# Second attention of a conv-attention network: scores computed a second time with keys on the partitions, exponentials summed in pairs

## The chip, the cores and the metric

The kernel runs as one program on one core of a Trainium2 chip. The metric is the time of one execution on the device in microseconds (us), as the median of several runs. PE is TensorE (matrix products), PEld its loading of weights, DVE is VectorE, ACT ScalarE, POOL GpSimd, and SP the engine that issues most transfers (its queue is SPq).

## What is computed

The input is x (2 images, 256 channels, 32x32 pixels, fp32). A first block (deformable attention and an MLP) gives a new x. The second block is plain multi-head attention over the 1024 pixels of an image, 8 heads of width 32, and it is the one that the change touches:

```python
def _L1_conv_ref(x, W_qkv, b_qkv, W_out, b_out):
    xf = jnp.transpose(x.reshape(B, C, N), (0, 2, 1))
    qkv = xf @ W_qkv + b_qkv
    qkv = qkv.reshape(B, N, N_HEADS, 3 * D_K)
    q, k, v = jnp.split(qkv, 3, axis=-1)
    attn = jnp.einsum('bihd,bjhd->bijh', q, k) * SCALE
    attn = jax.nn.softmax(attn, axis=2)
    res = jnp.einsum('bijh,bjhd->bihd', attn, v)
    res = res.reshape(B, N, N_HEADS * D_K)
    res = res @ W_out + b_out
    res = res + xf
```

Two images of eight heads give 16 heads (G), and the 1024 queries of a head are cut into 8 tiles of 128 rows (NK). One such tile of one head is a *unit*, so there are 128 units.

## The kernel before

Each engine has its own instruction list, written out by hand; semaphores order them across engines. An engine executes its list strictly in order, so what stands behind a waiting instruction waits too.

The second block runs in these steps. **Values:** PE makes V (L1026, 16 pieces) and DVE adds the bias and saves it (L741). **Projections:** PE makes Q and K in 8 pieces (L1038); ACT and DVE split each into two fp32r parts, high and low (L531, L767), and SP sends the parts to DRAM (`send_parts`, L299). Meanwhile DVE splits V into three 16-bit parts. **Head loads:** `load_head` (L303, L304) brings a head's parts back, stacked on the partitions in four groups of 32 rows (`Q_STACK`, `K_STACK`), so that one 128-row product sums high and low parts; eight transfers a head, into two buffers in turn.

**Units:** a loop of 8 rounds with 16 units each (PE: L1078). For a unit, PE computes the scores of 128 queries against 1024 keys into two PSUM banks (`scores`, L1047), DVE finds each row's negated maximum (`maxes`, L773), ACT takes the exponential with that maximum as its bias (`exps`, L535). The probabilities have queries on the partitions, and the product with V needs keys there, so PE transposes them (`turn`, L1055, eight 128x128 pieces). ACT and DVE copy them out of PSUM as two fp16 parts (L540, L543, L776, L779) and POOL makes one half of the low part (L390). PE multiplies both parts with V's three (`weigh`, L1063, 16 products); a column of ones beside V gives the sum. DVE inverts it (L786), ACT scales (L550), and POOL adds the three parts (L395, L397). The scores run three units ahead of the product with V.

**End:** PE transposes the results back to channels on the partitions (L1102), multiplies with W_out (L1113), DVE adds the residual (L814), SP stores.

## Time and profile before

| | |
|---|---|
| median of 3 runs | 1402.4 us (1402.36 to 1404.89) |
| the profiled execution | 1401.21 us |
| its span, first to last instruction | 1399.0 us |
| mean granted TensorE clock | 0.974 of full |
| busy: PE / PEld / DVE / ACT / POOL | 93% / 44% / 66% / 69% / 54% |

The span is what the trace shows, and the time of the same execution lies 2.2 us above it. Busy shares are averages over stages with different limits. A time of the trace is counted from the span's start. In rows of instructions, x8 is a merged group of 8, and a row's "idle before" names what ended the idle time. A product of two fp32 operands appears as two MATMUL records (L1038: 32 products in the code, x64 in the trace); a product of fp32r operands (L1047) or a transpose is one.

### The profile page before, as it was taken

How to read it: one execution, taken by the hardware profiler on the slowest of the kernel's cores; microseconds unless marked ns; L12 is line 12 of the kernel's file. 1: busy time of each engine (PE TensorE's matmuls, PEld its weight loads, DVE VectorE, ACT ScalarE, POOL GpSimd, SP SyncE). 2: the span in 40 equal slices, each digit the busy share in tenths (PEclk: the TensorE clock that was granted, in tenths of full speed). 3: DMA queues.
4: the chain of work that ended last, by engine and by line, in shares of the span. 5: the costliest groups of instructions: out<-in, count | busy, mean ns of one | idle time of the engine just before them, and what ended most of it. 6: DMA issues, size and time to landing. Idle time of an engine off the chain costs nothing.

```text
span 1399.0 us, 29958 instructions
## 1 busy us (share of the span) xinstructions
PE 1302.2 (93%) x11666; PEld 616.0 (44%) x11666; DVE 921.5 (66%) x1270; ACT 967.6 (69%) x1263; POOL 748.9 (54%) x681
## 2 busy tenths in 40 slices
PE   3169999999999999999999998799997999999998
PEld 2132222222222222222222226444454888888885
DVE  6876666666666666666666657410037999999995
ACT  3377777777777777777777773332204999999994
POOL 4166666666666666666666652200000767777772
PEclk9579999999999999999999999999999999999999
DMA  2141110111011101110111000000007222212211
GB/s 69 54 134 31 31 32 2 31 31 32 2 31 32 29 4 32 31 26 7 31 32 23 9 1 1 1 0 0 0 29 272 62 60 60 54 45 52 60 30 60
DMA packets 19922, 53.27 MB, mean 38 GB/s; under 512 B 4642, under 2 KB 7330, under 8 KB 19668
## 3 DMA queue, kind: packets, MB, share of 16 engines
q1 hardware_dynamic: 19824, 51.92, 14.1%
q8 instruction: 70, 1.15, 0.4%
q14 instruction: 24, 0.20, 0.0%
q10 hardware_dynamic: 4, 0.01, 0.0%
HBM read 40.95 MB, written 10.95 MB: 37 GB/s over the span
## 4 chain that ended last, share of the span: by engine, by line
PE 80%; DVE 11%; issue 3%; ACT 2%; POOL 2%; DMA 1%; SPq 1%; DVEq 0%; ACTq 0%; POOLq 0%
PE ps L898 31%; PE ps L907 17%; PE ps L889 5%; DVE aneg L773 5%; PE ps L1055 4%; PE ps L1063 4%; PE ps L1004 4%; PE ps L1014 4%; PE ps L1047 3%; DVE conv L620 2%; PE ps L1038 1%; DVE big L776 1%; POOL big L355 1%; PE ps L1026 1%; PE ps L991 1%
## 5 line engine op out<-in xcount | busy, mean ns | idle before, releaser
L898 PE MATMUL ps<-big,w 64*64 64x512 f32 x4096 | 483.5, 589 | 0.0
L479 ACT ACTIVATE big<-ps 128x1024 f32<-128x1024 f32 x256 | 262.0, 1023 | 179.0 <-PE ps L898 179.0
L674 DVE TENSOR_SCALAR big<-big 128x1024 f32<-128x1024 f32 x256 | 177.8, 694 | 263.8 <-POOL big L370 263.8
L668 DVE TENSOR_TENSOR big<-qpad,ps 128x1024 f32<-128x1024 f32 x256 | 311.0, 1215 | 7.8 <-ACT ps L458 5.4
L370 POOL TENSOR_TENSOR big<-qpad 128x1024 f32<-128x1024 f32 x128 | 244.5, 1910 | 133.2 <-PE ps L898 68.6
L370 POOL TENSOR_TENSOR big<-qpad,V 128x1024 f32<-128x1024 f32 x128 | 244.5, 1910 | 129.7 <-PE ps L898 73.5
L479 ACT ACTIVATE big<-ps,vec 128x1024 f32<-128x1024 f32 x256 | 284.0, 1109 | 0.0
L390 POOL TENSOR_TENSOR big<-BT,big 128x512 f16<-128x512 f32 x129 | 150.4, 1166 | 248.0 <-DVE big L776 248.0
L907 PE MATMUL ps<-big,w3s 128*32 128x512 f32 x2048 | 246.2, 598 | 1.3 <-ACT big L479 1.3
L898 PEld LDWEIGHTS ps<-big,w 64*64 64x64 f32 x4096 | 146.6, 133 | 205.9 <-issue 112.6
L773 DVE TENSOR_REDUCE aneg<-ps 128x1 f32<-128x1024 f32 x131 | 158.3, 1209 | 6.0 <-PE ps L1047 5.7
L535 ACT ACTIVATE big<-ps,aneg 128x1024 f32<-128x1024 f32 x130 | 148.5, 1142 | 6.0 <-DVE aneg L773 5.3
L1055 PE MATMUL ps<-ident,big 128*128 128x128 f32 x1032 | 136.3, 274 | 3.8 <-DVE big L779 3.8
L907 PEld LDWEIGHTS ps<-big,w3s 128*32 128x32 f32 x2048 | 53.5, 109 | 181.7 <-ACT big L479 92.2
L1055 PEld LDWEIGHTS ps<-ident,big 128*128 128x128 f32 x1032 | 121.1, 141 | 23.2 <-DVE big L779 5.7
L1063 PE MATMUL ps<-BT,big 128*128 x2048 | 115.6, 208 | 1.1
L1063 PEld LDWEIGHTS ps<-BT,big 128*128 128x128 f16 x2048 | 99.0, 97 | 21.3 <-issue 10.3
L889 PE MATMUL ps<-S,wl 57*64 57x512 bf16 x1024 | 102.3, 389 | 1.5 <-ACT vs L474 1.5
L1047 PE MATMUL ps<-h1l,h1h 128*128 128x512 f32 x262 | 94.5, 443 | 6.8 <-DMA h1l<-k_d 5.2
L889 PEld LDWEIGHTS ps<-S,wl 57*64 57x64 bf16 x1024 | 29.5, 105 | 144.7 <-ACT big L479 80.7
L779 DVE SCALAR_TENSOR_TENSOR big<-ps,big 128x512 f16<-128x512 f32 x129 | 89.1, 691 | 0.8 <-ACT big L543 0.4
L540 ACT ACTIVATE BT<-ps 128x512 f32<-128x512 f32 x129 | 79.1, 613 | 4.0 <-PE ps L1055 4.0
(140 smaller groups left out, 1116.5 us busy)
## 6 DMA issues: line engine op xcount, KB each, us to landing
raw<-s_f SPq DMA_DIRECT2D x32, 512.0 KB, 6.1
h1h<-q_d SPq DMA_DIRECT2D x64, 128.0 KB, 3.0
h1l<-k_d SPq DMA_DIRECT2D x64, 128.0 KB, 3.1
q_d<-XN SPq DMA_DIRECT2D x8, 512.0 KB, 2.6
k_d<-XN SPq DMA_DIRECT2D x8, 512.0 KB, 2.6
X<-in_x SPq DMA_DIRECT2D x2, 1024.0 KB, 6.3
out<-X SPq DMA_DIRECT2D x8, 256.0 KB, 2.0
m<-grid_d SPq DMA_DIRECT2D x1, 1024.0 KB, 4.6
```

Source lines behind the costliest of these rows:

```text
L370: pool.tensor_tensor(h1[m % HRING].rearrange("p (y a b) -> p y a b", y=2, b=W), u.unsqueeze(2).to_broadcast(shape), a[:, :, HALF // W * hf ...
L390: pool.tensor_tensor(PTL[u % 2][:, 0:HALF], PF[u % 2], PTH[u % 2][:, 0:HALF], ALU.subtract).then_inc(pFl_ready, 1)
L479: act.activation(h2[m % H2RING], z2[m % ZRING], ACT.Relu, bias=v("cb2") if m % 2 else 0.0).then_inc(h2_ready, 1)
L535: act.activation(PR[u % 2], bank(2 * (u % 2), 2), ACT.Exp, bias=aneg[u % 2][:, :]).then_inc(pr_ready, 1)
L668: dve.tensor_tensor(h1[m % HRING].rearrange("p (y a b) -> p y a b", y=2, b=W), u.unsqueeze(2).to_broadcast(shape), b[:, :, HALF // W * hf: ...
L674: dve.tensor_scalar(h1[m % HRING], h1[m % HRING], 0.0, None, ALU.max).then_inc(h1_ready, 1)
L773: dve.tensor_reduce(aneg[u % 2][:, :], bank(2 * (u % 2), 2), AX.X, ALU.max, negate=True).then_inc(mx_ready, 1)
L889: pe.matmul(z2[m % ZRING][CH * y:CH * (y + 1), HALF * x:HALF * (x + 1)], wl1[CH * x:CH * x + KROWS, 2 * w + y, :], S[CH * x:CH * x + KROWS ...
L898: last = pe.matmul(z2[m % ZRING][CH * y:CH * (y + 1), HALF * x:HALF * (x + 1)], w2[CH * x:CH * (x + 1), :], h1[m % HRING][CH * x:CH * (x + ...
L907: last = pe.matmul(zb[32 * k:32 * (k + 1), :], w3s[:, a:a + 32], h2[(m + k // 2) % H2RING][:, HALF * (k % 2):HALF * (k % 2 + 1)], start=(m ...
L1055: last = pe.transpose(bank(4 + hf)[:, P * i:P * (i + 1)], PR[u % 2][:, P * jt:P * (jt + 1)], ident[:, :])
L1063: last = pe.matmul(bank(6 + u % 2)[:, 0:VW], pT[u % 2][:, P * jt:P * (jt + 1)], V3[:, 2 * k + u // NK, jt, :], start=(jt == order[0] and p ...
```

## The change

The scores of a unit are now computed twice. `along(x)` computes them as before, queries on the partitions, only for the row maxima; its 128 queries are no longer consecutive but every eighth (`it:...:NK`), so that the maxima of a head lie in order in DRAM. POOL splits a head's maxima into two parts (`max_parts`), and SP moves them through DRAM into two more rows beneath the head's Q (`move_max`: a transfer out, a wait for it, a transfer in). K has ones in these two rows. `across(s)` then computes the scores with keys on the partitions, 128 keys against 1024 queries, and the two rows subtract each query's maximum within the product. ACT takes the exponential, which needs no transpose. PE multiplies V, as 32 columns, with it, in four products side by side, one for each quarter of the queries (`weigh`). POOL adds the exponentials of two units (`added`), and PE multiplies the sum with ones, again in four (`sums`). DVE divides once a head (`divide`), and SP puts the result in place (`place_head`, four transfers). All is fp32 there, without 16-bit parts.

The stack of a head's parts has three groups instead of four (the product of the two low parts is left out), so `load_head` issues six transfers. Q and K have three buffers (`HEADS3`) instead of two. `along` runs 13 units ahead (`AHEAD_MAX`) of `across` and has one pair of PSUM banks (0 and 1); `across` alternates between two pairs. The values are made between the first eight `along` and no longer before the projections. V's parts, the transposes, and the copies out of PSUM are gone. The loops are written out.

```diff
+        QS = [h1h[:, 2 * i:2 * i + 2, :].rearrange("p a b -> p (a b)") for i in range(2)] + [qk3[:, 0, :]]
+        KS = [h1l[:, 2 * i:2 * i + 2, :].rearrange("p a b -> p (a b)") for i in range(2)] + [qk3[:, 1, :]]
+        PT = [big[:, 4 + i, :] for i in range(PRING)]
+        PSUMS = [big[:, 11, :], BT[:, 14:16, :].rearrange("p a b -> p (a b)")]
+        OT = [big[:, 10, QUARTER * i:QUARTER * (i + 1)] for i in range(2)]
+        orec = [big[:, 10, QUARTER * i:QUARTER * (i + 1)] for i in (2, 3)]
...
+            def load_head(n):
+                i = n % HEADS3
+                for r in range(len(Q_STACK)):
+                    sp.dma_start(QS[i][D * r:D * (r + 1), :].bitcast(fp32), q_d[Q_STACK[r], D * n:D * (n + 1), :]).then_inc(st_in[i], 16)
+                    sp.dma_start(KS[i][D * r:D * (r + 1), :].bitcast(fp32), k_d[K_STACK[r], D * n:D * (n + 1), :]).then_inc(st_in[i], 16)
+
+            def move_max(n):
+
+                sp.wait_ge(m_lo, n + 1)
+                sp.dma_start(m_d[n].rearrange("a (q t) -> q a t", t=NK), mparts[n % HEADS3][:, :, :].bitcast(fp32)).then_inc(m_out, 16)
+                sp.wait_ge(m_out, 16 * (n + 1))
+                sp.dma_start(QS[n % HEADS3][ROWS:ROWS + 2, :].bitcast(fp32), m_d[n]).then_inc(m_in, 16)
+
+            def place_head(n):
+
+                sp.wait_ge(o_done, n + 1)
...
+                for c in range(4):
+                    sp.dma_start(rT[row:row + D, t, QUARTER * c:QUARTER * (c + 1)], OT[n % 2][D * c:D * (c + 1), :]).then_inc(rT_in, 16)
+
+            for n in range(4):
...
+                sp.wait_ge(parts_out[i], 32 * 2)
+            for n in range(HEADS3):
+                load_head(n)
+            for n in range(4, 2 * T):
                 send_parts(n)
             for i in range(2):
                 sp.wait_ge(parts_out[i], 32 * T)
-            with sp.Fori(0, G // 2 - 1) as k:
-                sp.wait_ge(sc_ready, UNITS * k + NK)
-                load_head(0, 2 * k + 2)
-                sp.wait_ge(sc_ready, UNITS * k + 2 * NK)
-                load_head(1, 2 * k + 3)
-            sp.wait_ge(sc_ready, UNITS * (G // 2 - 1) + NK)
-            sp.sem_inc(st_in[0], 16 * 2 * HP)
+            move_max(0)
+            for n in range(1, G):
+                if n + 2 < G:
+                    if n >= 2 or n + 2 >= HEADS3:
+                        sp.wait_ge(st_ready, NK * (n + 2 - HEADS3 + 1))
+                    load_head(n + 2)
+                move_max(n)
+                place_head(n - 1)
+            place_head(G - 1)
...
+            def max_parts(n):
+
+                pool.wait_ge(mx_ready, NK * (n + 1))
+                if n >= HEADS3:
+                    pool.wait_ge(m_out, 16 * (n - HEADS3 + 1))
+                hi, lo = (mparts[n % HEADS3][:, a, :] for a in range(2))
+                pool.tensor_copy(hi, amax[n % HEADS3][:, :]).then_inc(m_hi, 1)
+                pool.wait_ge(m_hi, n + 1)
+                pool.tensor_tensor(lo, amax[n % HEADS3][:, :], hi.bitcast(fp32), ALU.subtract).then_inc(m_lo, 1)
+
+            max_parts(0)
+            for j in range(SLOTS // 2):
+                if j % 4 == 1 and j // 4 + 1 < G:
+                    max_parts(j // 4 + 1)
+                pool.wait_ge(pr_ready, 2 * j + 2)
+                if j >= 2:
+                    pool.wait_ge(sums_done, j - 1)
+                pool.tensor_tensor(PSUMS[j % 2], PT[2 * j % PRING], PT[(2 * j + 1) % PRING], ALU.add).then_inc(added, 1)
...
+            for s in range(SLOTS):
+                act.wait_ge(st_ready, s + 1)
+                if s >= PRING:
+                    act.wait_ge(pv_done, s - PRING + 1)
+                    act.wait_ge(added, (s - PRING) // 2 + 1)
+                act.activation(PT[s % PRING], bank(2 + 2 * (s % 2), 2), ACT.Exp).then_inc(pr_ready, 1)
...
+
+            def maxes(x):
+
+                n, it = x // NK, x % NK
+                dve.wait_ge(sc_ready, x + 1)
+                if it == 0 and n >= HEADS3:
+                    dve.wait_ge(m_lo, n - HEADS3 + 1)
+                dve.tensor_reduce(amax[n % HEADS3][:, it:it + 1], bank(0, 2), AX.X, ALU.max, negate=True).then_inc(mx_ready, 1)
+
+            def divide(n):
+
+                dve.wait_ge(pv_done, NK * (n + 1))
+                dve.wait_ge(sums_done, NK // 2 * (n + 1))
+                dve.reciprocal(orec[n % 2], bank(6 + n % 2)[:, QUARTER:2 * QUARTER]).then_inc(rec_done, 1)
+                dve.wait_ge(rec_done, n + 1)
+                if n >= 2:
+                    dve.wait_ge(rT_in, 64 * (n - 1))
+                dve.tensor_tensor(OT[n % 2], bank(6 + n % 2)[:, 0:QUARTER], orec[n % 2], ALU.mult).then_inc(o_done, 1)
...
-                v_part(n % 4, n // 4)
...
+            for x in range(NK):
+                value(2 * x)
+                value(2 * x + 1)
+                maxes(x)
+            for x in range(NK, SLOTS + 2 * NK + 1):
+                if x < SLOTS:
+                    maxes(x)
+                n = (x - NK - AHEAD_MAX - 3) // NK
+                if n >= 0 and (x - NK - AHEAD_MAX - 3) % NK == 0:
+                    divide(n)
...
+            def along(x):
+
+                n, it = x // NK, x % NK
+                if it == 0:
+                    pe.wait_ge(st_in[n % HEADS3], 96 * (n // HEADS3 + 1))
+                if x >= 1:
+                    pe.wait_ge(mx_ready, x)
+                for hf in range(2):
+                    last = pe.matmul(bank(hf), QS[n % HEADS3][0:ROWS, it:it + NK * (P - 1) + 1:NK],
+                                     KS[n % HEADS3][0:ROWS, HALF * hf:HALF * (hf + 1)], start=True, stop=True)
                 last.then_inc(sc_ready, 1)
...
+            def across(s):
+
+                n, kt = s // NK, s % NK
+                if kt == 0:
+                    pe.wait_ge(m_in, 16 * (n + 1))
+                if s >= 2:
+                    pe.wait_ge(pr_ready, s - 1)
+                for hf in range(2):
+                    last = pe.matmul(bank(2 + 2 * (s % 2) + hf), KS[n % HEADS3][0:ROWS + 2, P * kt:P * (kt + 1)],
+                                     QS[n % HEADS3][0:ROWS + 2, HALF * hf:HALF * (hf + 1)], start=True, stop=True)
+                last.then_inc(st_ready, 1)
+
+            def weigh(s):
+
+                n, kt = s // NK, s % NK
+                if kt == 0 and n >= 2:
+                    pe.wait_ge(o_done, n - 1)
+                pe.wait_ge(pr_ready, s + 1)
+                for c in range(4):
+                    last = pe.matmul(bank(6 + n % 2)[D * c:D * (c + 1), 0:QUARTER], V[:, n, kt, :],
+                                     PT[s % PRING][:, QUARTER * c:QUARTER * (c + 1)],
+                                     start=(kt == 0), stop=(kt == NK - 1), skip_group_check=True)
+                last.then_inc(pv_done, 1)
+
+            def sums(j):
+
+                n = j // (NK // 2)
+                pe.wait_ge(added, j + 1)
+                for c in range(4):
+                    last = pe.matmul(bank(6 + n % 2)[D * c:D * (c + 1), QUARTER:2 * QUARTER], ones[:, :],
+                                     PSUMS[j % 2][:, QUARTER * c:QUARTER * (c + 1)],
+                                     start=False, stop=(j % (NK // 2) == NK // 2 - 1), skip_group_check=True)
+                last.then_inc(sums_done, 1)
...
+            for x in range(NK):
+                value(2 * x)
+                value(2 * x + 1)
+                along(x)
+            for x in range(NK, AHEAD_MAX):
+                along(x)
+            pe.wait_ge(vv_saved, 2 * NK)
+            pe.wait_ge(ones_ready, 1 + HEADS3)
+            for s in range(SLOTS + 4):
+                if s < SLOTS:
+                    across(s)
+                if s + AHEAD_MAX < SLOTS:
+                    along(s + AHEAD_MAX)
+                if s % 2 == 1:
+                    if 0 <= s - 3 < SLOTS:
+                        weigh(s - 3)
+                        weigh(s - 2)
+                    if s >= 5:
+                        sums((s - 5) // 2)
+
...
-                pe.wait_ge(rT_saved, 4 * b + 4)
+                if n % 4 == 0:
+                    pe.wait_ge(rT_in, 64 * NH * (b + 1))```

**PE, two steps around a head's start.** The list before has, for each unit, two score products, eight transposes, and 16 products with V:

```order
L1047 MATMUL ps<-h1l,h1h 128x512 [waits pr_ready]
L1047 MATMUL ps<-h1l,h1h 128x512
L1055 MATMUL ps<-ident,big 128x128 [waits pF_ready]
L1055 MATMUL ps<-ident,big 128x128 x3
L1055 MATMUL ps<-ident,big 128x128 [waits pTl_ready]
L1055 MATMUL ps<-ident,big 128x128 x3
L1063 MATMUL ps<-BT,big 128x97 [waits pFl_ready,oo_saved]
L1063 MATMUL ps<-BT,big 128x97 x15
```

Now there are these (L1010 is `across`, L998 `along`, L1021 `weigh`, L1031 `sums`), here from the last unit of the second head to the first of the third (`qk3` is the third buffer of Q and K):

```order
L1010 MATMUL ps<-h1h,h1l 128x512 [waits pr_ready]
L1010 MATMUL ps<-h1h,h1l 128x512
L998 MATMUL ps<-h1l,h1h 128x512 [waits mx_ready]
L998 MATMUL ps<-h1l,h1h 128x512
L1021 MATMUL ps<-big 32x256 [waits pr_ready]
L1021 MATMUL ps<-big 32x256 x3
L1021 MATMUL ps<-big 32x256 [waits pr_ready]
L1021 MATMUL ps<-big 32x256 x3
L1031 MATMUL ps<-BT,ones 32x256 [waits added]
L1031 MATMUL ps<-BT,ones 32x256 x3
L1010 MATMUL ps<-qk3 128x512 [waits pr_ready,m_in]
L1010 MATMUL ps<-qk3 128x512
```

The products with V and those with ones stand in every second step only, and the first `across` of a head waits for `m_in`, the landing of that head's maxima.

**SP, one head in the loop.** Before, a head's loads wait for the scores of an earlier head (`sc_ready`):

```order
L303 ISA [waits sc_ready]
L303 DMA h1h<-q_d 32x1024
L304 DMA h1l<-k_d 32x1024
L303 DMA h1h<-q_d 32x1024
L304 ISA
L304 DMA h1l<-k_d 32x1024
L303 DMA h1h<-q_d 32x1024
L304 DMA h1l<-k_d 32x1024
L303 DMA h1h<-q_d 32x1024
L304 DMA h1l<-k_d 32x1024
```

Now, for n = 2 (L300 and L301 load head 4, L306 and L308 move the maxima of head 2, L315 places head 1):

```order
L300 DMA h1h<-q_d 32x1024 [waits st_ready]
L301 DMA h1l<-k_d 32x1024
L300 DMA h1h<-q_d 32x1024
L301 DMA h1l<-k_d 32x1024
L300 DMA h1h<-q_d 32x1024
L301 DMA h1l<-k_d 32x1024
L306 DMA m_d<-mparts2 128x2x8 [waits m_lo]
L308 DMA qk3<-m_d 2x1024 [waits m_out]
L315 DMA XN<-big 32x256 [waits o_done]
L315 DMA XN<-big 32x256 x3
```

The loads now wait for `st_ready`, all `across` of the head before (n - 1), and the two transfers of head n's maxima stand behind them on SP.

## Rows read from the trace of the kernel before

**Rows 1.** The cores: the profiled execution's span and clock

```profile
core 0: 1399.0 us, clock 0.974
```

**Rows 2.** Windows of the second block: busy time by engine, clock, DMA share, GB/s

```profile
1027.00:1041.20 14.20, 14.09 (x65) 12.47 (x66) 6.42 (x16) 0.00 (x0) 0.00 (x0) 1.00 0.00 0
1041.20:1068.70 27.50, 27.45 (x64) 11.83 (x63) 20.28 (x15) 7.80 (x8) 0.00 (x0) 1.00 0.59 235
1080.80:1378.30 297.50, 290.19 (x3327) 250.37 (x3325) 285.27 (x513) 287.27 (x513) 209.37 (x385) 1.00 0.21 52
1378.30:1382.00 3.70, 3.67 (x33) 3.68 (x34) 0.00 (x0) 2.98 (x7) 0.00 (x0) 1.00 0.00 0
1382.00:1399.00 17.00, 13.78 (x33) 5.78 (x31) 6.00 (x8) 1.04 (x3) 0.00 (x0) 0.97 0.33 124
```

**Rows 3.** Timeline of one unit: start, duration, engine, line

```profile
1096.68 0.71 PE L1047 MATMUL ps<-h1l,h1h 128*128 128x512 f32 x2
1096.85 1.15 ACT L535 ACTIVATE big<-ps,aneg 128x1024 f32<-128x1024 f32 x1
1097.22 1.03 PE L1055 MATMUL ps<-ident,big 128*128 128x128 f32 x8
...
1098.19 0.87 PE L1063 MATMUL ps<-BT,big 128*128 x16
...
1098.88 0.71 PE L1047 MATMUL ps<-h1l,h1h 128*128 128x512 f32 x2
```

**Rows 4.** Timeline where a maximum waited for its scores

```profile
1101.53 0.72 PE L1047 MATMUL ps<-h1l,h1h 128*128 128x512 f32 x2
...
1102.29 1.22 DVE L773 TENSOR_REDUCE aneg<-ps 128x1 f32<-128x1024 f32 x1 [0.31 <-PE ps L1047]
```

**Rows 5.** Timeline of the first block: four products side by side, twice

```profile
500.52 1.92 PE L907 MATMUL ps<-big,w3s 128*32 128x512 f32 x16
...
502.37 0.41 PE L889 MATMUL ps<-S,wl 57*64 57x512 bf16 x4
```

**Rows 6.** Groups of instructions: count, busy us, mean ns of one

```profile
L390 POOL TENSOR_TENSOR big<-BT,big 128x512 f16<-128x512 f32 x129 | 150.4, 1166 | 248.0 <-DVE big L776 248.0
...
L786 DVE RECIPROCAL arec<-ps 128x1 f32<-128x1 f32 x128 | 20.2, 158 | 0.0
...
L713 DVE RECIPROCAL srec<-ssum 128x8 f32<-128x8 f32 x16 | 3.1, 196 | 0.0
```

**Rows 7.** Timeline of SP: first and sixth load of a head

```profile
1109.04 0.32 SPq L303 DMA_DIRECT2D h1h<-q_d  x1
...
1111.35 0.37 SPq L304 DMA_DIRECT2D h1l<-k_d  x1
```

**Rows 8.** Issues of transfers: KB each, median us from issue to landing

```profile
h1l<-k_d SPq DMA_DIRECT2D x64, 128.0 KB, 3.1
...
s_d<-qpad SPq DMA_DIRECT2D x3, 64.0 KB, 2.1
...
grid_d<-gxy SPq DMA_DIRECT2D x1, 8.0 KB, 2.5
```

**Rows 9.** The chain that ended last, before the first scores: start, us

```profile
1064.29 2.63 DMA k_d<-XN
...
1066.97 0.35 SPq L303
...
1070.15 3.60 DMA h1l<-k_d
```

**Rows 10.** Windows of 1 us around PE's longest gap there

```profile
1068.00:1069.00 1.00, 0.66 (x2) 0.00 (x0) 0.83 (x1) 0.31 (x1) 0.00 (x0) 1.00 0.76 250
...
1073.00:1074.00 1.00, 0.12 (x1) 0.15 (x1) 0.33 (x1) 0.00 (x0) 0.00 (x0) 0.81 1.09 238
1074.00:1075.00 1.00, 1.00 (x3) 0.81 (x4) 0.00 (x0) 0.00 (x0) 0.00 (x0) 0.50 1.03 201
...
1080.00:1081.00 1.00, 1.00 (x7) 0.87 (x6) 0.45 (x2) 0.74 (x3) 0.11 (x1) 0.77 1.01 414
```

More of the change, by code:

```diff
@@ L79, in build @@
         k_d = dram("k_d", [2, G * D, N], fp32)
+        m_d = dram("m_d", [G, 2, N], fp32)
         vec = sb("vec", [P, NVEC])
@@ L200, in build @@
-        rT_ready, rT_saved, fin_ready, fin_saved, stored = (
-            sem(x) for x in ("rT_ready", "rT_saved", "fin_ready", "fin_saved", "stored"))
+        st_in = [sem(f"st_in{i}") for i in range(HEADS3)]
+        added, sums_done = sem("added"), sem("sums_done")
+        m_hi, m_lo, m_out, m_in, rT_in, ones_ready = sem("m_hi"), sem("m_lo"), sem("m_out"), sem("m_in"), sem("rT_in"), sem("ones_ready")
+        sc_ready, mx_ready, st_ready, pr_ready, pv_done, o_done = (
+            sem(x) for x in ("sc_ready", "mx_ready", "st_ready", "pr_ready", "pv_done", "o_done"))
@@ new lines, in _ @@
+            pool.wait_ge(ones_ready, 1)
+            for i in range(HEADS3):
+                pool.tensor_copy(KS[i][ROWS:ROWS + 2, :], ones[ROWS:ROWS + 2, 0:1].to_broadcast((2, N))).then_inc(ones_ready, 1)
+            pool.wait_ge(ones_ready, 1 + HEADS3)
+            def max_parts(n):
[6 more added lines that the diff above has]
+                pool.tensor_tensor(lo, amax[n % HEADS3][:, :], hi.bitcast(fp32), ALU.subtract).then_inc(m_lo, 1)
@@ L736, in _, with value @@
                     dve.scalar_tensor_tensor(xs, bank(4 + r % 4), v("mlp_b2", ct), xs, ALU.add, ALU.add).then_inc(x2_ready, 1)
-            for n in range(2 * NK):
+            def value(n):
                 b, jt = n // NK, n % NK
@@ L1058, in weigh @@
-            def weigh(u, k):
-                order = list(range(4, NK)) + list(range(4))
-                for jt in order:
-                    for pT in (PTH, PTL):
-                        last = pe.matmul(bank(6 + u % 2)[:, 0:VW], pT[u % 2][:, P * jt:P * (jt + 1)],
-                                         V3[:, 2 * k + u // NK, jt, :],
-                                         start=(jt == order[0] and pT is PTH), stop=(jt == order[-1] and pT is PTL))
-                last.then_inc(oo_ready, 1)
```

223 lines of the change are left out of this document (28 added, 195 removed).

## The prediction

> **What bounds the kernel now.** I read the windows first, to see which part of the span the change can touch. The values take 14.2 us, the projections 27.5, and the loop of units 297.5 from 1080.8; then come 3.7 of transposes and 17.0 of output [rows 2]. The rest, the first block, stays. In the loop PE, DVE and ACT are each busy for at least 285 of 297.5 us, POOL for 209: three engines are full at once. The timeline of one unit shows why. PE starts its scores at 1096.68, the transposes 0.54 later, the product with V 0.97 later still, and the next scores 0.69 after that, so a unit is 2.20 us [rows 3]. With the restarts of the loop it is some 2.3 (128 units in 297.5, the first ones earlier).
>
> **The new pace between heads.** PE's work for two steps (two units), from these rows. Two score products cost 0.54 from start to next start [rows 3], so `across` or `along` is 0.54. For `weigh` and `sums` the nearest row is L907, also four fp32 products of 32 columns side by side: eight products with 512 moving columns take 1.85 us to the next group (500.52 to 502.37) [rows 5], or 0.23 each. Here the moving operand has 256 columns, which I cost at half, 0.116. Two `weigh` and one `sums` are 12 such, 1.39 us. PE in all: 4 x 0.54 + 1.39 = 3.55 for two steps.
>
> But `along` has one pair of banks, so the next one waits for the maximum of the last. Scores take 0.72 until DVE starts, the reduction 1.22, with 0.04 at each hand-over [rows 4]: 2.02 us from one `along` to the next where PE has nothing longer to do. In the step without `weigh` PE has 0.54 + 0.54, so 2.02 holds. In the other it has 0.54 + 1.39 + 0.54 = 2.47, longer than 2.02. Two steps: 4.49, or 2.25 us a unit.
>
> The other engines stay below: ACT has one exponential of 1.15 a unit [rows 3]. POOL adds 1024 columns once in two units; L390 does 512 in 1.17 us [rows 6], so about 2.3 of the 4.49. DVE divides once a head. A 256-column reciprocal isn't in the trace: 1 column costs 158 ns, 8 cost 196 [rows 6], 5.4 ns a column, so 1.5 us at most and some 0.4 at least (256 columns at DVE's pace of 1024 in 1.22, plus its floor). With the product of 0.4 it starts when its step's maximum ends and delays the next by 0 to 0.9; I take 0.4, or 5 us for 13 heads.
>
> **Start and end.** The projections start at 1027.1 now and end at 1054.6. SP issues the 18 loads of three heads before the last two pairs of parts. A piece is 3.44 (27.5 / 8). Before, piece 5 left PE at 1061.8 (1041.2 + 6 x 3.44) and the first load was issued at 1066.97 [rows 9], 5.1 later. Now piece 3 leaves PE 13.8 after the start, at 1040.9, the loads begin at 1046.0, and 18 issues at 0.46 (2.31 / 5) [rows 7] end near 1054.4. Pieces 6 and 7 wait on ACT for the parts after that, so the last low part is ready at about 1062.5, and PE idles 8 us, against 5.2 before. The first eight `along` are interleaved with 16 values: 16 x 0.88 (14.09 of PE for 16) [rows 2] + 8 x 0.54 = 18.4, 2 more at the low clock; five more `along` at 2.02 are 10.1. `across(0)` is at 1093. Then 115 steps with `along` ahead of them, 115 x 2.25 = 258: 1351. The 13 last have PE's 0.54 + 0.70 = 1.25 each, 16: 1367. The last exponential, sum and product are about 4. With divisions (5) and a late maximum of head 15 (2, see below) the output products start at 1378; the 3.7 of transposes fall away, and 17.0 remain [rows 2]. The first four output products hide the last division and `place_head`. **Without what follows, the span would be 1395**, 4 below the 1399.0 [rows 1].
>
> **The wait that is new.** `across(8n)` needs `m_in`. Head n's maxima are found five steps earlier, but SP is by then in its wait for `st_ready`, all `across` of head n-1, since the loads of head n+2 stand ahead of `move_max(n)`. So everything follows the end of `across(8n-1)`:
> - six issues of loads: 2.31 us from the first to the sixth [rows 7], the transfer out issued at 2.8;
> - it lands 2.1 to 2.5 later [rows 8] if alone, but the last load, issued at 2.3, lands 3.1 [rows 8] to 3.6 [rows 9] after that, on the same queue. I take 5.7;
> - the transfer in, issued 0.05 us after the landing (as the load at 1066.97 after the one that landed at 1066.92 [rows 9]), 2.1: 7.8, and PE resumes at 8.0.
>
> Without the wait `across(8n)` would start 2.7 after the end of `across(8n-1)` (that ends at 1.26 in its step, `along` starts at 2.02, then 0.54 + 1.39). So PE stalls 5.3 us. Behind `across(8n)` in its list stand the next `along`, hence DVE, and all `weigh`; the lead of 13 units doesn't help, since nothing passes. It happens for n = 1 to 13, the heads with loads ahead of their maxima: 13 x 5.3 = 69.
>
> **The clock.** PE was idle from 1068.7 to 1073.9; the granted clock fell from 1.00 to 0.50 (2.4 to 1.2 GHz) within 1073 to 1074 and returned in 1080 to 1081 after 5 us of work with a pause [rows 10]. The stall of 5.3 is as long as that gap. At the low level, `across` and `along` cost twice, a loss of 1 to 2.5 us until it is back; since not every stall need end in a fall, I take 1.2 each, 16 in all. The Trainium skill (TensorE: Matmul & The Clock Gate, "Loop structure matters more than you think") warns of just this, a wait for DMA between bursts of products that recurs and starts each burst at the low rate. The trace agrees for its one gap (0.50 in 1074). By the rule each of the 13 stalls pays in full, which would make 13 x 2 = 26 of my 16.
>
> **The sum.** 1395 + 69 + 16 = 1480 of span. The profiled execution is 2.2 above its span and the median 1.2 above that: 3.4. Predicted 1483 us, against 1402.4.
>
> **Bounds.** Per head: with the shortest issues and landings (2.8 + 2.1 + 0.1 + 2.0, the transfer out not held by the loads) PE resumes at 7.0, stalls 4.3 and keeps its clock: 56. With both landings at 3.6 behind the last load's, it resumes at 2.3 + 3.6 + 0.1 + 3.6 = 9.6, stalls 6.9 and loses 2.5: 122. The rest of the span: 1387 (nothing for divisions, start and tail as short as before) to 1410 (0.9 a division, 0.1 more a step). So 1446 to 1535; I give 1446 to 1524.
>
> **The rivals.**
> - *The maxima arrive in time* (the other side). If the way from `st_ready` to `m_in` takes under 2.7 us, PE sees nothing of it, and the kernel is at 1395 + 3.4 = 1398, 0.3% faster. For it: three full engines are relieved. Against: two landings in sequence are 4.2 at the least [rows 8], and six issues 2.3. It could be only if the queue order on SP were not what I read. To be merely even, the stalls would have to sum to 4 us, 0.3 a head. 9%.
> - *Weights read with a step.* `along` takes every eighth column of Q as weights, 32 bytes apart; no weights with such a step are in the trace. If PE has to wait 0.1 for each of the two weight loads, 0.2 is added to each of 128 `along` (0.72 [rows 4] before), which is on the maximum's path: +26 at most, less in the PE-bound step: 1483 + 20 = 1503. The Trainium skill (SBUF — State Buffer, on SBUF's 16-byte lines) says that access to a new line each time pays a penalty. No run here shows it yet. 12%.
> - *The clock stays low.* PE is busy 3.55 of 4.49 us; if with a stall each 8 units the clock did not return, the two steps would take about 2.5 + 4.9 and the span grow by 160, to about 1645. Against: in [rows 10] it returned within 7 us, with a pause. 4%.
> - *The forecast*, stalls at 13 heads with the clock partly lost, 1483: 73%. The remaining 2% are for no change.
>
> **Chances.** No change is within 0.2% (2.8 us), about what this kernel's measurement can tell. Faster 0.09, same 0.02, slower 0.89. The two slower rivals lie inside or above the range: it holds the forecast and most of the second.
>
> **What the profile will show.** Right: 13 gaps of 4 to 7 us on PE before L1010, released by the transfer of `m_d`, 8 steps apart; a granted clock below 1 after them; 2.2 to 2.3 us a unit between them; SP issuing L306 right behind six loads. Wrong: PE idle before L1010 under 1 us (the first rival); L998 records much longer than 0.71 a pair (the second); 0.23 rather than 0.12 us for a product of L1021, which would put some 60 us more on PE; or POOL's sums above 4.5 us, so that PE waits for `added`.

## The result, and the profile after

The changed kernel takes **1531.56 us** (median of 4, 1530.53 to 1541.78), the kernel before 1402.46 (median of 4). The ratio is 1.0932, with a 95% interval of 1.0885 to 1.098. I had said 1483, with a range that ended at 1524: the direction held, the time lies 49 us above the forecast and outside the range. The profiled execution has a span of 1529.8 us at a mean clock of 0.929, against [rows 1].

First the waits of PE from 1040 us on, in the changed kernel: how long in all, how often, the longest.

```profile
PE ps L998 <- DVE amax L727: 65.6, 64, 1.9
PE ps L1010 <- DMA h1h<-m_d: 44.8, 10, 4.8
PE ps L1010 <- DMA qk<-m_d: 17.9, 4, 4.7
PE ps L986 <- DVE XN L744: 11.2, 1, 11.2
```

The second and third line are waits for the maxima: 14 gaps before `across`, 62.7 us together. Thirteen of them, 58.8 us, are the stalls of the forecast (heads 1 to 13, 4.2 to 4.8 us each). The last, 3.9 us, is the late maximum of head 15, for which the forecast had 2. Then a window of 50 us in the loop, where the kernel before had a clock of 1.00 [rows 2]. The columns are the busy time of PE, PEld, DVE, ACT and POOL, the granted clock, the DMA share and GB/s:

```profile
1150.00:1200.00 50.00, 33.37 (x219) 18.94 (x208) 20.84 (x18) 14.02 (x14) 17.34 (x11) 0.80 0.13 30
```

DVE and ACT, full before, are busy 42% and 28% of it. PE is busy for 33 of 50 us, some of it at half clock. SyncE's queue at one head, start and duration:

```profile
1147.80 0.32 SPq L300 DMA_DIRECT2D h1h<-q_d  x1
...
1150.02 0.42 SPq L301 DMA_DIRECT2D h1l<-k_d  x1
1150.48 0.42 SPq L306 DMA_DIRECT2D m_d<-mparts  x1
1153.92 0.24 SPq L308 DMA_DIRECT2D qk<-m_d  x1
```

Six loads come first (2.68 us to the issue of L306), then 3.44 until the transfer in can be issued, and PE resumes at 1155.41, 7.6 after the first load was issued; the forecast had 8.0. Two misses nearly cancel in this: the transfer out holds the next for 3.44 (2.9 in the forecast), and from the issue of the transfer in to PE it is 1.49 (2.2). The period of a head, from one resumption of PE to the next, is in the timeline of PE:

```profile
1155.41 1.22 PE L1010 MATMUL ps<-qk 98*128 98x512 f32 x2 [4.50 <-DMA qk<-m_d]
...
1166.01 0.85 PE L998 MATMUL ps<-h1l,h1h 96*128 96x512 f32 x2 [0.94 <-DVE amax L727]
...
1171.83 0.87 PE L998 MATMUL ps<-h1l,h1h 96*128 96x512 f32 x2 [1.92 <-DVE amax L727]
1172.62 1.07 PE L1021 MATMUL ps<-big 128*32 128x256 f32 x16
...
1174.06 0.74 PE L1010 MATMUL ps<-qk 98*128 98x512 f32 x2
1174.64 0.65 PE L998 MATMUL ps<-h1l,h1h 96*128 96x512 f32 x2
...
1176.60 0.87 PE L998 MATMUL ps<-h1l,h1h 96*128 96x512 f32 x2 [0.85 <-DVE amax L727]
...
1183.54 1.22 PE L1010 MATMUL ps<-h1h,h1l 98*128 98x512 f32 x2 [4.64 <-DMA h1h<-m_d]
```

This period is 1183.54 - 1155.41 = 28.1 us for 8 units; the mean of the twelve from 1126.82 to 1456.39 is 27.5, where the forecast had 24.9. The kernel before took 18.5 a head (first loads at 1164.87 and, two heads on, at 1201.84). At full clock two steps are 4.77 (1171.83 to 1176.60); the pair with the division is 1.05 longer (1166.01 to 1171.83 is 5.82); the stall is 4.6. Four pairs, division and stall are 19.1 + 1.05 + 4.6 = 24.8. The other 3.3 us (2.8 in the mean period, with its stall of 4.5) are what is left, and I put them down to the clock. Windows at two stalls, first of 1 us, then of the stretches at either level:

```profile
1154.00:1155.00 1.00, 0.00 (x0) 0.00 (x0) 0.00 (x0) 0.00 (x0) 0.00 (x0) 0.51 0.03 8
...
1164.00:1165.00 1.00, 1.00 (x4) 0.49 (x3) 0.36 (x1) 0.98 (x1) 1.00 (x1) 0.87 0.00 0
...
1154.00:1164.00 10.00, 8.13 (x35) 4.50 (x36) 2.45 (x2) 2.09 (x3) 1.06 (x1) 0.50 0.00 1
1164.00:1181.00 17.00, 11.19 (x94) 6.54 (x93) 9.44 (x8) 5.95 (x6) 8.39 (x6) 0.99 0.23 55
1181.00:1192.00 11.00, 8.00 (x36) 4.47 (x37) 2.45 (x2) 2.12 (x3) 1.34 (x2) 0.53 0.00 1
```

The granted clock is at its lower level, 1.2 GHz, for 10 of 28 us, though PE works for 8 of these 10. In the gap of [rows 10] it was back 7 us after it fell. At other heads the first product still runs at full clock, and the fall comes right behind it:

```profile
1211.33 0.73 PE L1010 MATMUL ps<-h1h,h1l 98*128 98x512 f32 x2 [4.70 <-DMA h1h<-m_d]
```

```profile
1211.00:1212.00 1.00, 0.67 (x3) 0.63 (x4) 0.00 (x0) 0.00 (x0) 0.00 (x0) 1.00 0.00 0
1212.00:1213.00 1.00, 1.00 (x4) 0.87 (x3) 0.13 (x1) 0.91 (x1) 0.00 (x0) 0.52 0.00 0
```

In windows of 1 us over the whole loop, every one of the 14 gaps is followed by the lower level: for 6.8 us at eight of them, for 10.2 us at six. The pause behind the division (1.92 us, as at 1171.83) is followed by it at one of 13 heads, for 3.4 us from 1143.

The groups of instructions of `along`'s weight loads and DVE's reciprocal:

```profile
L998 PEld LDWEIGHTS ps<-h1l,h1h 96*128 96x128 f32 x176 | 50.6, 328 | 71.5 <-DVE amax L727 54.4 <-issue 13.8
...
L733 DVE RECIPROCAL big<-ps 128x256 f32<-128x256 f32 x14 | 24.6, 1758 | 4.7 <-PE ps L1031 4.7
```

A weight load of `along`, every eighth column, takes 328 ns. The reciprocal of 256 columns takes 1.76 us, above the 1.5 that I had as its most.

### The profile page after: what moved, and what is told of

Its sections match the earlier page's. It is cut to its first block, busy times and chain, and to the rows that moved or that the text cites. A ratio compares the mean times of both kernels' runs of the same rounds, so it can differ in the third digit from the quotient of the medians.

```text
span 1529.8 us, 24649 instructions
## 1 busy us (share of the span) xinstructions
PE 1307.2 (85%) x10340; PEld 531.1 (35%) x10340; DVE 808.6 (53%) x905; ACT 800.7 (52%) x867; POOL 697.3 (46%) x395
## 3 DMA queue, kind: packets, MB, share of 16 engines
q8 instruction: 82, 1.34, 0.4%
## 4 chain that ended last, share of the span: by engine, by line
PE 77%; DVE 9%; DMA 5%; SPq 3%; POOL 2%; issue 1%; ACT 1%; POOLq 0%; DVEq 0%; ACTq 0%
PE ps L845 29%; PE ps L854 16%; PE ps L998 5%; PE ps L836 5%; DVE amax L727 4%; PE ps L1021 4%; PE ps L951 4%; PE ps L961 4%; PE ps L1010 3%; DMA m_d<-mparts 3%; DVE big L596 2%; PE ps L1031 2%; SPq L301 2%; DVE big L733 2%; SPq L300 1%
## 5 line engine op out<-in xcount | busy, mean ns | idle before, releaser
L490 ACT ACTIVATE big<-ps 128x1024 f32<-128x1024 f32 x256 | 261.9, 1023 | 179.0 <-PE ps L845 179.0
L383 POOL TENSOR_TENSOR big<-qpad 128x1024 f32<-128x1024 f32 x128 | 244.5, 1910 | 133.0 <-PE ps L845 69.5
L550 ACT ACTIVATE big<-ps 128x1024 f32<-128x1024 f32 x128 | 127.4, 1024 | 314.6 <-PE ps L1010 314.3
L727 DVE TENSOR_REDUCE amax<-ps 128x1 f32<-128x1024 f32 x128 | 156.6, 1224 | 220.1 <-PE ps L998 219.6
L421 POOL TENSOR_TENSOR big<-big 128x1024 f32<-128x1024 f32 x32 | 76.0, 2374 | 195.3 <-PE ps L1031 180.1
L998 PE MATMUL ps<-h1l,h1h 96*128 96x512 f32 x176 | 77.2, 526 | 46.1 <-DVE amax L727 46.1
L1010 PE MATMUL ps<-h1h,h1l 98*128 98x512 f32 x176 | 72.3, 502 | 44.8 <-DMA h1h<-m_d 44.8
L421 POOL TENSOR_TENSOR BT<-big 128x1024 f32<-128x1024 f32 x32 | 75.4, 2357 | 62.7 <-PE ps L1031 61.5
L1021 PE MATMUL ps<-big 128*32 128x256 f32 x1024 | 81.7, 445 | 0.0
L998 PEld LDWEIGHTS ps<-h1l,h1h 96*128 96x128 f32 x176 | 50.6, 328 | 71.5 <-DVE amax L727 54.4
L1010 PEld LDWEIGHTS ps<-h1h,h1l 98*128 98x128 f32 x176 | 37.3, 235 | 71.4 <-DMA h1h<-m_d 49.6
## 6 DMA issues: line engine op xcount, KB each, us to landing
h1h<-q_d SPq DMA_DIRECT2D x33, 128.0 KB, 3.0
h1l<-k_d SPq DMA_DIRECT2D x33, 128.0 KB, 3.0
```

What stands on the lines that cost most here:

```text
L383: pool.tensor_tensor(h1[m % HRING].rearrange("p (y a b) -> p y a b", y=2, b=W), u.unsqueeze(2).to_broadcast(shape), a[:, :, HALF // W * hf ...
L421: pool.tensor_tensor(PSUMS[j % 2], PT[2 * j % PRING], PT[(2 * j + 1) % PRING], ALU.add).then_inc(added, 1)
L490: act.activation(h2[m % H2RING], z2[m % ZRING], ACT.Relu, bias=v("cb2") if m % 2 else 0.0).then_inc(h2_ready, 1)
L727: dve.tensor_reduce(amax[n % HEADS3][:, it:it + 1], bank(0, 2), AX.X, ALU.max, negate=True).then_inc(mx_ready, 1)
L998: last = pe.matmul(bank(hf), QS[n % HEADS3][0:ROWS, it:it + NK * (P - 1) + 1:NK], KS[n % HEADS3][0:ROWS, HALF * hf:HALF * (hf + 1)], start ...
L1010: last = pe.matmul(bank(2 + 2 * (s % 2) + hf), KS[n % HEADS3][0:ROWS + 2, P * kt:P * (kt + 1)], QS[n % HEADS3][0:ROWS + 2, HALF * hf:HALF ...
```

## The experiments

All kernels are edits of the changed one; a ratio is to the kernel before on the same chip, with its 95% interval. The kernel before took 1404.3 us beside experiments 1 to 4, 1402.3 beside 5, 6, 8 and 11, and 1403.5 beside 7, 9 and 10, so a difference between experiments of two of these groups is good to some 2 us.

**1. The maxima first.** On SyncE, `move_max(n)` is issued ahead of the wait for `st_ready` and the loads.

```diff
             for n in range(1, G):
+                move_max(n)
                 if n + 2 < G:
...
                     load_head(n + 2)
-                move_max(n)
                 place_head(n - 1)
```

> The changed kernel with one edit on SP: the two transfers of head n's maxima are issued before SP waits for the loads of head n+2, no longer behind them. Theory (order on SP makes the stall): the 13 gaps of 4.5 to 4.8 us before the first transposed-score product of a head go, and with them the half clock behind each (about 3.3 us); 13 x (4.6 + 3.3) = 103 less, so about 1428 us, granted clock near 0.97. Rival 1 (the two transfers are themselves too slow, wherever they are issued): gaps of several us stay, over 1480. Rival 2 (the clock is low because of PE's own 75% load, not of the gaps): the gaps go, the clock stays near 0.85 in the second attention, about 1531 - 60 = 1470.

Measured: 1457.4 us (1454.64 to 1458.99), ratio 1.0377 [1.0354, 1.0401]; clock 0.947. Of the waits for `m_d` one is left, 4.1 us at the last head:

```profile
PE ps L998 <- DVE amax L727: 69.5, 64, 1.9
...
PE ps L1010 <- DMA h1h<-m_d: 4.1, 1, 4.1
```

So the order on SyncE made the stalls, and it cost 74 us. The busy time of PE, from the pages of the changed kernel and of this one, splits them:

```profile
PE 1307.2 (85%) x10340; PEld 531.1 (35%) x10340; DVE 808.6 (53%) x905; ACT 800.7 (52%) x867; POOL 697.3 (46%) x395
```

```profile
PE 1286.8 (88%) x10340; PEld 523.9 (36%) x10340; DVE 808.8 (56%) x905; ACT 800.4 (55%) x867; POOL 698.8 (48%) x395
```

The same 10340 records of products take PE 20 us less, which is the clock, and the other 54 of the 74 are idle time (59 less before `across`, 4 more for the maxima). But I had expected 1428. The windows of this kernel show why it isn't there. PE pauses for 1.92 us behind the division, from 1158.6 to 1160.53:

```profile
1159.00:1160.00 1.00, 0.00 (x0) 0.00 (x0) 1.00 (x2) 0.67 (x1) 0.53 (x1) 1.00 0.00 0
1160.00:1161.00 1.00, 0.47 (x1) 0.47 (x2) 0.47 (x1) 0.00 (x0) 0.00 (x0) 0.91 0.13 33
1161.00:1162.00 1.00, 1.00 (x6) 0.29 (x9) 0.22 (x1) 0.00 (x0) 0.00 (x0) 0.50 0.25 62
...
1164.00:1165.00 1.00, 1.00 (x11) 0.61 (x4) 0.00 (x0) 0.00 (x0) 0.40 (x1) 0.88 0.02 8
```

Behind it the clock is at 0.50 for three windows, without any stall by DMA. Of the 13 such pauses nine were followed by a fall, of 3.4 or 6.8 us, and four by none.

**2. PE kept at work in the stall.** 12 products whose result nobody reads stand ahead of `across(8n)`, behind a wait for the maxima.

```diff
             for s in range(SLOTS + 4):
+                if s % NK == 0 and 0 < s < NK * (G - 2):
+                    pe.wait_ge(mx_ready, s + AHEAD_MAX)
+                    for _ in range(12):
+                        pe.matmul(bank(0), KS[...][0:ROWS, 0:P], QS[...][0:ROWS, 0:HALF], start=True, stop=True)
                 if s < SLOTS:
                     across(s)
```

> The changed kernel, with the stall left as it is, but PE fills it: before the first transposed-score product of heads 1 to 13 it waits for the last maximum and then makes 12 products of 512 columns into the bank of the row maxima, whose results nobody uses. If the half clock costs what I read (3.3 us a head), the clock stays at full and the time falls by up to 43 us, to about 1489, though 12 products were added. Rival (the halved clock costs little, as the predicted 1.2 a head): 1515 or above. If filling is no help at all because the products outlast the gap: above 1531.

Measured: 1529.09 us (1523.11 to 1531.57), ratio 1.0878 [1.0844, 1.0911]; no gain that can be told from nothing. The timeline of PE in this kernel (L1049 are the added products):

```profile
1182.33 3.04 PE L1049 MATMUL ps<-h1h,h1l 96*128 96x512 f32 x12
1186.45 0.74 PE L1010 MATMUL ps<-h1h,h1l 98*128 98x512 f32 x2 [1.09 <-DMA h1h<-m_d]
...
1199.65 0.87 PE L998 MATMUL ps<-qk 96*128 96x512 f32 x2 [1.93 <-DVE amax L727]
...
1201.55 1.10 PE L1031 MATMUL ps<-big,ones 128*32 128x256 f32 x8
```

With work in the gap the clock stays full through it: `across` at 1186.45 takes 0.74, not 1.22, and so it is at 12 of the 13 filled gaps. It then falls within the head, at the division's pause: the sums at 1201.55 take 1.10 in place of 0.61. In most heads it falls a second time, some 2 us behind the resumption. By windows of 1 us the lower level still takes 7.1 us a head, against 8.5 in the changed kernel. Single heads take 25.6 to 28.7 us from one resumption to the next, their mean is 27.4 (twelve, from 1129.48 to 1458.03), the same as in the changed kernel. So the idle stall is not the only thing that brings the clock down. My 1489, which gave all of the fall to it, fell. The rival's number, 1515 or above, came true, but the run doesn't test its reason (that the halved clock costs little), since the clock still fell.

**3. Neighbouring columns as weights.** As experiment 1, and `along` reads 128 consecutive queries (each maximum then goes to another row than its own).

```diff
-                    last = pe.matmul(bank(hf), QS[n % HEADS3][0:ROWS, it:it + NK * (P - 1) + 1:NK],
+                    last = pe.matmul(bank(hf), QS[n % HEADS3][0:ROWS, P * it:P * (it + 1)],
```

> Kernel a_max_first, and the row-maxima products take 128 neighbouring columns of Q as weights and not every eighth; the maxima are then not those of the queries they are subtracted from (only the time counts). Theory (weights read with a step load slowly: 328 against 194 ns a load): two such products fall from 0.84 to 0.71 us, a pair of steps from 4.77 to about 4.5 us, 57 pairs: 15 us below a_max_first. Rival (the time of a pair is set elsewhere): within 3 us of a_max_first.

Measured: 1444.49 us (1442.01 to 1446.82), ratio 1.0285 [1.0261, 1.0309], 13 below experiment 1. The weight load falls to 206 ns:

```profile
L998 PEld LDWEIGHTS ps<-h1l,h1h 96*128 96x128 f32 x154 | 28.2, 206 | 66.4 <-DVE amax L727 50.6 <-issue 12.6
```

The step between columns costs 0.12 us a load and 13 us in all (15 expected). That is the second rival of the prediction, real, but half of the 26 that I had as its most.

**4. No reciprocal.** As experiment 1, with a copy in its place, so that the output is multiplied by the sums and not divided.

```diff
-                dve.reciprocal(orec[n % 2], bank(6 + n % 2)[:, QUARTER:2 * QUARTER]).then_inc(rec_done, 1)
+                dve.tensor_copy(orec[n % 2], bank(6 + n % 2)[:, QUARTER:2 * QUARTER]).then_inc(rec_done, 1)
```

> Kernel a_max_first with the reciprocal of 128x256 in each head's division replaced by a copy of the same size (so the output is multiplied by the sum and not divided). Theory (1.76 us of reciprocal holds the next maximum up and with it PE, about 1.05 us a head): 13 us below a_max_first. Rival (DVE has slack, the delay is taken back): within 3 us of a_max_first.

Measured: 1421.73 us (1418.14 to 1425.25), ratio 1.0118 [1.0095, 1.0141], 36 below experiment 1. PE's waits for the maxima fall by 13 (69.5 to 56.6), which is what I had expected of the whole:

```profile
PE ps L998 <- DVE amax L727: 56.6, 64, 1.4
```

The larger part of the rest is the clock. The two profiled executions are 32 us apart, and the same 10340 records of products take PE 18 us less (1286.8 to 1268.8); the other 14 are idle time. The windows of 1150 to 1350 of the kernels of experiment 1 and of this one:

```profile
1150.00:1350.00 200.00, 158.45 (x1216) 94.41 (x1216) 111.77 (x94) 73.84 (x76) 92.10 (x58) 0.94 0.17 43
```

```profile
1150.00:1350.00 200.00, 163.26 (x1341) 99.96 (x1340) 112.19 (x106) 82.70 (x84) 102.60 (x64) 1.00 0.19 48
```

Without the long pause the clock is 1.00 throughout, although PE still waits 0.85 to 0.95 us in each pair.

**5. No reciprocal, stalls left.** The same edit on the changed kernel itself.

> The changed kernel, stalls left in, with the reciprocal of 128x256 replaced by a copy of the same size. In a_max_first the same edit took off 36 us where 13 were expected, and the clock went from 0.86-0.97 to 1.00: theory, part of the half clock comes from the 1.9 us pause that the reciprocal makes, not from the stall. Then here it takes off only the 1.05 us a head (13 to 17 us, about 1515), since the stall makes the clock fall anyway. Rival (the reciprocal costs 2.7 us a head by itself): about 1495.

Measured: 1520.84 us (1517.49 to 1524.23), ratio 1.0841 [1.0806, 1.0876], 11 below the changed kernel, clock 0.927. PE's waits for the maxima fall by 15 (65.6 to 50.9), which is all that the edit gives. While the stalls are there they bring the clock down anyway. From 1150 to 1350 it is 0.81, where the changed kernel has 0.85, and the lower level behind a stall lasts 10.2 us at 11 of 13 heads, against six of 13. The two causes don't add.

**6. One `weigh` a step.** As experiment 1, and `weigh` is spread evenly in place of two in each odd step.

```diff
-                if s % 2 == 1:
-                    if 0 <= s - 3 < SLOTS:
-                        weigh(s - 3)
-                        weigh(s - 2)
-                    if s >= 5:
-                        sums((s - 5) // 2)
+                if 0 <= s - 2 < SLOTS:
+                    weigh(s - 2)
+                if s % 2 == 1 and s >= 5:
+                    sums((s - 5) // 2)
```

> Kernel a_max_first, with one product with V in each step instead of two in every second step (the sums stay in every second). Theory: PE's work of a step then is 1.8 and 2.25 us, and the path along - maximum is 2.17, so two steps take about 4.4 instead of 4.77 us: 20 us less, 1437. Rival (each switch between whole-array products and four side by side costs): no gain, 1457 or above.

Measured: 1433.36 us (1433.16 to 1436.37), ratio 1.0218 [1.0191, 1.0245], 24 below experiment 1. The waits for the maxima fall from 69.5 to 25.2. As the change has it, `along` waits in one step while PE has too much to do in the other.

**7. The start.** As experiment 6; only head 0 is loaded before the last parts are sent.

```diff
-            for n in range(HEADS3):
-                load_head(n)
+            load_head(0)
             for n in range(4, 2 * T):
                 send_parts(n)
+            for n in range(1, HEADS3):
+                load_head(n)
```

> The maxima first on SyncE, one unit of products with the values per step, and at the start only head 0 loaded before the last parts are sent. The run with the first two edits took 1433.4 us, and TensorE waited about 11 us before the products with the values at its start; with the start edit in another kernel this wait fell to 3.9 us. Theory: 1433.4 - 7 = 1426 us. Rival (the wait at the start is given back, since the maxima of head 0 are then late or the first products come at a falling clock): 1433 us.

Measured: 1427.61 us (1423.47 to 1429.79), ratio 1.0177 [1.0154, 1.0199], 6 below experiment 6. PE's wait at L986 falls from 11.4 to 4.0. The timeline and a window of this kernel show what I had not expected:

```profile
1204.87 0.87 PE L999 MATMUL ps<-h1l,h1h 96*128 96x512 f32 x2 [1.15 <-DVE amax L728]
```

```profile
1206.00:1207.00 1.00, 1.00 (x16) 0.39 (x8) 1.00 (x1) 0.00 (x0) 0.00 (x0) 0.50 0.26 65
```

The pause behind the division is now 1.15 us, the longest from 1120 to 1380, and at nine of its 13 heads the clock falls behind it for 3.4 us. PE is busy for 241 of these 260 us. In experiment 4 it is busy for 213 of them, waits up to 0.95 us in each pair, and keeps its clock.

**8. The reciprocal in two halves.** As experiment 7; each half of the reciprocal stands behind a maximum of its own, and the multiplication behind a third (during the last eight steps, all at once).

```diff
+            def invert(n, h):
+                half = QUARTER // 2
...
+                dve.reciprocal(orec[n % 2][:, half * h:half * (h + 1)],
+                               bank(6 + n % 2)[:, QUARTER + half * h:QUARTER + half * (h + 1)]).then_inc(rec_done, 1)
...
+                if x < SLOTS and n >= 0 and late < 3:
+                    (lambda m: invert(m, 0), lambda m: invert(m, 1), scale)[late](n)
```

> Kernel e_first_spread, with the reciprocal cut into two halves that lie behind two maxima and the multiplication behind a third, and with only head 0 loaded before the last parts are sent (heads 1 and 2 after them). Theory: no maximum is held up for more than 0.3 us, so the 36 us that d_first_no_reciprocal gained come back, and PE's idle time before the values falls from 11.2 to about 7: 1437 - 36 - 4 = about 1397, granted clock near 0.97. Rival (the clock falls for other reasons): above 1415.

Measured: 1462.65 us (1459.71 to 1466.7), ratio 1.0429 [1.04, 1.0458], far above the 1397 that I had expected. The waits before `across` are back, in 14 heads (here L1021 is `across`, L315 `place_head`):

```profile
1261.37 2.42 SPq L315 DMA_DIRECT2D XN<-big  x4
1263.84 0.58 SPq L306 DMA_DIRECT2D m_d<-mparts  x1
1267.26 0.25 SPq L308 DMA_DIRECT2D qk<-m_d  x1
```

```profile
1268.83 0.95 PE L1021 MATMUL ps<-qk 98*128 98x512 f32 x2 [3.68 <-DMA qk<-m_d]
```

The gaps are 39 us together. The multiplication comes two maxima later; SyncE waits for it in `place_head(n-1)`, and the next `move_max` stands behind. It is the fault of the changed kernel once more, made by my own edit: a wait on an in-order queue ahead of what is needed first.

**9. The placing later.** As experiment 8, with `place_head` one iteration later.

```diff
             for n in range(1, G):
                 move_max(n)
+                if n >= 2:
+                    place_head(n - 2)
...
                     load_head(n + 2)
-                place_head(n - 1)
+            sp.wait_ge(rT_in, 64 * (G - 2))
+            place_head(G - 2)
             place_head(G - 1)
```

> As the kernel above, with the reciprocal in two halves behind two maxima and the multiplication behind a third, and with the placing of a head put one iteration later on SyncE, behind the next head's maxima. In the kernel with the halves but the old place, the placing waited for the late multiplication and the maxima queued behind it came about 4 us late. Theory: that wait is gone; TensorE's longest pause by VectorE is about 1 us, the clock stays at full in the middle, and the time falls below 1426 by half to all of the 36 us that the reciprocal cost in the kernels with the maxima first: 1390 to 1408 us. Rival A (the gap before the products across comes back from another queue): 1450 us or more. Rival B (the pauses add up the same however they are cut, and the clock still falls): 1420 us or more.

Measured: **1391.57 us** (1390.88 to 1393.56), ratio 0.9919 [0.99, 0.9939]: 0.8% faster than the kernel before, 71 below experiment 8 and 36 below experiment 7. PE's longest waits from 1040 us on, then a window of the loop:

```profile
PE ps L1012 <- DVE amax L731: 10.3, 21, 1.4
PE ps L1000 <- DVE XN L754: 4.1, 1, 4.1
```

```profile
1250.00:1300.00 50.00, 48.80 (x371) 26.03 (x371) 32.91 (x32) 22.83 (x23) 27.48 (x18) 1.00 0.22 57
```

In experiment 7 the same waits were 25.2 in 34 and 3.3 for `m_d`, and the clock 0.88 to 0.97 in the windows from 1100 on. So 18 us of waiting are gone (25.2 - 10.3 + 3.3). The profiled executions are 33 us apart: 17 are idle time of PE, and 16 are busy time for the same products (1302.5 to 1286.9), the clock. Its SyncE issues the maxima of a head every 17.6 us, so a unit takes 2.20, against 2.31 before:

```profile
1192.63 0.38 SPq L306 DMA_DIRECT2D m_d<-mparts  x1
1194.20 0.24 SPq L308 DMA_DIRECT2D h1h<-m_d  x1
...
1210.22 0.38 SPq L306 DMA_DIRECT2D m_d<-mparts  x1
```

The transfer out, with no load in front, lets the next be issued after 1.57 us, not 3.44.

**10. Plain weights on top.** As experiment 9, with the edit of experiment 3 (maxima at other rows than their own).

> As the kernel above, and the weights of the first scores are 128 neighbouring columns and no longer every eighth (the maxima then stand at other rows than they belong to; the output is another). In the earlier pair this took 13 us. If TensorE sets the pace of all steps now: 13 to 15 us below the kernel above. If VectorE's maxima set the pace instead: 0 to 5 us below it.

Measured: 1381.09 us (1379.18 to 1382.96), ratio 0.984 [0.9819, 0.9862]. 10.5 less, nearer to the 13 to 15 that I had for a pace set by PE than to the 0 to 5 for one set by DVE. The weight loads of `along` take 198 ns in place of 329. It is a bound for a kernel that gets its maxima into order in another way.

**11. Plain weights, order restored in the transfer.** As experiment 8, and the maxima are put into order as they are written to DRAM, in pieces of 4 bytes.

```diff
-                sp.dma_start(m_d[n].rearrange("a (q t) -> q a t", t=NK), ...
+                sp.dma_start(m_d[n].rearrange("a (t q) -> q a t", t=NK), ...
```

> Kernel i_spread_halves, with neighbouring columns of Q as weights in the row-maxima products, and the maxima put in order by their transfer to DRAM (2048 pieces of 4 bytes). Theory: the load's step is gone, 0.13 us an along on the path of the maximum, 57 x 0.28 = 15 us less, about 1382, if the transfer of small pieces still lands within the five steps (11 us) that it has. Rival: it takes longer than that, a gap before each head returns, above 1400.

Measured: 1577.13 us (1574.9 to 1580.44), ratio 1.123 [1.1202, 1.1258], 114 above experiment 8, where I had expected some 1382. A transfer of `m_d` takes 10.1 us to its landing, for 8 KB:

```profile
m_d<-mparts SPq DMA_DIRECT2D x16, 8.0 KB, 10.1
```

PE waits 160 us for it in 15 gaps. The strided weights of the changed kernel cost 0.12 us a load to avoid this, and avoid it well.

## Why the prediction was wrong

**The mechanism was right.** The new stall is at the place, by the releaser and with the order of issues that I had described: 7.6 us from the first load to PE's resumption (8.0 in the forecast, with the two misses that nearly cancel), 4.5 of stall (5.3), and experiment 1 takes 74 us away by moving one line. Of the 69 us 59 came at these 13 heads.

**Where the 49 us are.** By the forecast the first stall ends at 1093 + 18 + 5.3 = 1116, twelve periods of 24.9 lead to 1415, and the output products start at 1463. In the trace these are 1126.8, 1456.4 and 1512.5: 10 us too little before the first stall, 31 in the twelve periods, 8 after the last. In a period the 2.6 missed are: clock +1.6, pairs +1.1, division +0.7, stall -0.8.

**The step that failed is the clock,** "a loss of 1 to 2.5 us until it is back; since not every stall need end in a fall, I take 1.2 each, 16 in all". It is 2.8 in the mean period, 37 over 13 heads, and above the most that I had allowed. Both reasons for the small number failed. The first was that not every stall need end in a fall: all 14 gaps did. The second was the length. I had the clock return after 5 us of work, as in [rows 10], and it stayed low for 6.8 us at eight gaps and for 10.2 at six. The single gap of [rows 10] was followed by another stretch of work than this one, and I carried its length over. Why it is the longer stretch at some heads stays open. The Trainium skill (TensorE: Matmul & The Clock Gate, "Loop structure matters more than you think") warns that such a loop restarts each burst at the low rate. The trace agrees at all fourteen gaps; at five of them the product that resumed still took 0.73 to 0.74, as at full clock, and the fall came within about 1 us. By the 2 us that I had worked out for the rule the term would be 26, still too little.

**Three other terms** were low, each by its own working:
- Two steps: 4.49 in the forecast, 4.77 measured. The odd step is 2.81 in place of 2.47, the even one 1.96 in place of 2.02. In the odd step a pair of `along` takes 0.87 and not 0.71, and the 24 records of `weigh` and `sums` 1.44 (1172.62 to 1174.06) against 1.39. Experiment 3 gives 13 us back by the weights alone. The Trainium skill (SBUF — State Buffer, "Specifications (TRN2)") says that access pays a penalty each time it crosses to a new 16-byte line; the load is 328 ns at a step of 32 bytes and 206 at neighbours, so the trace agrees. I held this as a rival at +20 when it belonged in the sum as a term of its own.
- The division: 0.4 a head in the forecast, 1.05 measured. The reciprocal is 1.76 us, 6.9 ns a column: the slope of 5.4 from [rows 6] was a fair guide, but "I take 0.4" sat below the middle of my bounds of 0 to 0.9, and the measured delay lies above both.
- The start: the last low part was ready at 1067.5, not at 1062.5, as the part sent behind the 18 loads took 5.98 us to land; PE idled 11.2 us, not 8. `across(0)` came at 1099.7, not at 1093, and the clock, at 2 us in the forecast, was low for longer: it was at its lower level until 1072, and again from 1093 to 1113, while five `along` in a row each waited 1.3 to 1.4 us for a maximum. Experiments 1, 4, 5, 7, 8 and 9 show the same stretch, for 20 to 27 us.

```profile
1093.00:1113.00 20.00, 14.90 (x40) 7.97 (x41) 9.04 (x8) 4.09 (x4) 5.10 (x4) 0.50 0.00 0
```

**The range** ended at 1524 although the bounds that I had worked out reached 1535. It had 2.5 us a head as the most for the clock, and the measured mean passes that.

**The rivals.** The maxima did not come in time; the clock did return in each head; both fell. The sums on POOL took 2.4 us, as estimated, and PE did not wait for them in the loop. That the division could bring down the clock by itself was no rival of mine at all. Experiments 1 and 4 show it, some 18 to 23 us, but once the stalls are gone: in the changed kernel it did so at one head only.

**What the change is worth.** Freed of the order on SyncE, of the uneven steps, of the long pauses and of the loads at the start, the new form takes 1391.6 us, 0.8% less than before. Its pace is 2.20 us a unit against 2.31. The work that it takes off ACT, DVE and POOL buys little, because PE was full beside them, and the scores are computed twice.

## What to carry to other kernels

On a queue that works in order, put first what the next critical step waits for: a wait for a buffer to come free, and the loads behind it, belong after the small transfer on which TensorE depends. When a change relieves three engines and leaves a fourth full, look for what it adds to the fourth. Cost a pause of TensorE together with the clock that follows it: in the kernel of experiment 1, a reciprocal that made a pause of 1.9 us once a head cost 36 us, more of it by the clock than by waiting. Cut in two pieces, with the placing moved out of the way, it left pauses of 0.2 us and a clock of 1.00 in the loop from 1120 us on (experiment 9).
